# One more level of static start-up: every preparation part as a table step, first key stacks from GpSimd, chunk 0's gate later

## The reference

```
x += (softmax((LN(x) Wq + bq)(ctx Wk + bk)^T / sqrt(32)) (ctx Wv + bv)) Wo + bo      # 16 heads of 32
chosen = argmax(LN(x) gate_w^T)                                                     # 8 experts
x += LN(x) expert_w[chosen]^T
```

## Time and profile before

| | us |
|---|---|
| median of three runs | 1016.04 |
| lowest, highest | 1012.83, 1017.89 |
| profiled execution | 1020.97 |
| its span, first to last instruction | 1019.2 |

### The profile page before, as it was taken

One profiled execution on the slowest core, in us unless ns is written; L12 is line 12 of the kernel. 1 busy time (PEld: TensorE's weight loads), 2 busy tenths in 40 slices (PEclk: granted clock), 3 DMA queues, 4 the chain that ended last, 5 costly groups with the idle time before them and its releaser, 6 DMA issues. The chain is left out here.

```text
span 1019.2 us, 27541 instructions
## 1 busy us (share of the span) xinstructions
PE 922.2 (90%) x8838; PEld 549.9 (54%) x8839; DVE 793.0 (78%) x1828; ACT 558.6 (55%) x928; POOL 540.9 (53%) x553
## 2 busy tenths in 40 slices
PE   5759699999989999989999999999783999999996
PEld 3234555655556555655566555656662555555553
DVE  7746888998979889888899998978876556565663
ACT  4355476776847768658686686774833112121210
POOL 3022445456454654645556555464443577777774
PEclk9877799999989999989999999999886999999998
DMA  9211134244342441533414343224624355555550
GB/s 319 76 41 33 33 95 136 53 135 109 86 135 59 136 136 45 141 82 114 140 43 134 86 119 116 61 75 139 228 108 153 110 166 175 160 169 170 167 179 26
DMA packets 82792, 119.52 MB, mean 117 GB/s; under 512 B 22001, under 2 KB 47141, under 8 KB 82671
## 3 DMA queue, kind: packets, MB, share of 16 engines
q1 hardware_dynamic: 69935, 81.87, 29.9%
q0 software_dynamic: 11664, 36.05, 9.3%
q10 hardware_dynamic: 1072, 0.02, 0.1%
HBM read 55.24 MB, written 38.13 MB: 92 GB/s over the span
## 5 line engine op out<-in xcount | busy, mean ns | idle before, releaser
L527 POOL TENSOR_TENSOR p_lo<-pf,p_hi 77x512 f16<-77x512 f32 x128 | 151.7, 1191 | 222.3 <-ACT p_hi L1085 221.9
L1084 ACT ACTIVATE pf<-scoresT,exp_scale 77x512 f32<-77x512 f32 x256 | 175.2, 684 | 85.6 <-PE scoresT L818 78.3
L1567 PE MATMUL mo<-e_w,x2T_hi 128*128 x576 | 184.4, 382 | 0.7 <-DVE x2T_lo L1604 0.7
L1085 ACT ACTIVATE p_hi<-scoresT,exp_scale 77x512 f16<-77x512 f32 x256 | 175.6, 686 | 0.0
L1587 ACT ACTIVATE x2T_hi<-mt 128x512 f16<-128x512 f32 x72 | 43.1, 598 | 183.5 <-PE mt L1556 183.5
L1614 DVE SCALAR_TENSOR_TENSOR res<-mo,inv,row 128x512 f32<-128x512 f32 x72 | 54.0, 750 | 91.1 <-PE mo L1567 88.9
L527 DVE TENSOR_TENSOR p_lo<-pf,p_hi 77x512 f16<-77x512 f32 x128 | 109.5, 871 | 11.0 <-ACT p_hi L1085 9.5
L1172 DVE TENSOR_REDUCE negmax<-work 128x4 f32<-128x308 f32 x256 | 112.4, 467 | 0.4 <-PE work L870 0.3
L1567 PE MATMUL mo<-e_w,x2T_lo 128*128 x288 | 109.9, 382 | 0.0
L1538 POOL DMA_INDIRECT out<-res,row x72 | 71.5, 994 | 65.0 <-DVE xn L1599 56.8
L790 PE MATMUL work<-xnT_hi,wq_hi 128*128 128x512 f16 x256 | 99.1, 387 | 4.3 <-DVE xnT_lo L1150 2.5
(11 more groups left out here) (256 smaller groups left out, 2205.1 us busy)
## 6 DMA issues: line engine op xcount, KB each, us to landing
row<-rows_by_expert SPq DMA_DIRECT2D x72, 257.5 KB
q_st<-q_hi SPq DMA_DIRECT2D x256, 64.0 KB, 2.0
xt<-in_x SPq DMA_DIRECT2D x15, 1024.0 KB, 8.6
q_st<-q_lo SPq DMA_DIRECT2D x128, 64.0 KB, 2.0
ebuf<-in_L_ffn_expert_w SPq DMA_DIRECT2D x14, 512.0 KB, 7.4
er<-in_L_ffn_expert_w SPq DMA_DIRECT2D x7, 1024.0 KB, 15.1
out<-res,row POOLq DMA_INDIRECT x72, 2.7
xt<-in_x SPq DMA_DIRECT2D x4, 256.0 KB, 6.2
```

Of the source, the lines that this page charges most:

```text
L527: return tt.tensor_tensor(pp[1][0:LK, g % 2, j, :], pf[:, j, :], pp[0][0:LK, g % 2, j, :], ALU.subtract)
L1084: nc.scalar.activation(pf[:, j, :], sbank[n % SB][0:LK, :], ACT.Exp, scale=exp_scale[0:LK, :])
L1085: nc.scalar.activation(pp[0][0:LK, g % 2, j, :], sbank[n % SB][0:LK, :], ACT.Exp, scale=exp_scale[0:LK, :]).then_inc(sem("exp_done"), 1)
L1567: ins = nc.tensor.matmul(obank2[u % 2][:, :], x2T[ia][:, u % 2, k, :], w, start=k == 0 and n == 0, stop=k == KT - 1 and n == 2)
```

## The change

- `prologue()` of TensorE, VectorE and ScalarE is cut into steps (CX, K, CG; Z, VC, KZ, GM, GT, CM, CB, BQ, ST, SA, MQ, MK, MA; PZ, CA, KE, XN) that stand in new tables of iteration -1 among the old ones. GpSimd gets LN, VO, KD in iteration -1 and TR (tables of ranks) in 0.
- The tables of iterations -1 and 0 are new in their order. DV2/DV3, CV move from -1 to 0 (VectorE), BV, WO0, EX0, EX1 from 0 to -1 (ScalarE).
- The gate of chunk 0, before GX in iteration -1, is GY, the first step of iteration 0.
- The stacked keys of batch 0 are issued by GpSimd (KD, behind F), and query pair 1 of chunk 0 by SyncE behind nmT's DMA of iteration 0.
- `ln` makes rstd first and std last, by a multiplication; GX and GY wait for it (`std_ready`).
- e_sum has sixteen columns, EM is gone; one reduction over sixteen columns stands in H of iteration 13.

```diff
-    M12 V00 V01 O2 M13 B2 Q2 R EM0 V10 V11 M20 SL P30 Q3 V20 M21 M22 M23 V21 P31 O3 M30 B3 GX VE V30 M31 M32 M33 V31
+    M12 V00 V01 O2 M13 B2 Q2 R V10 V11 M20 SL P30 Q3 V20 M21 M22 M23 V21 P31 O3 M30 B3 GX VE V30 M31 M32 M33 V31
...
 STEPS_FIRST = order("""
-    T0 T1 AT T2 T3 AB DV1 Q0 DV2 Q1 M00 M01 M02 M03 BT Q2 M10 M11 M12 M13 BB Q3 M20 M21 M22 M23 DV3 GX M30 M31 M32 M33
+    CX0 CX1 K0 K1 K2 K3 T0 AT T1 T2 AB CG DV0 T3 DV1 Q0 BT M00 M01 Q1 M02 DV2 M03 M10 M11 BB Q2 Q3 M12 M13 M20 DV3 M21
+    M22 M23 M30 M31 M32 M33
 VECTOR_FIRST = order("""
-    T0 T1 AR T2 T3 AS WQ0 WQ1 WQ2 WQ3 KL Q0 OM0 OM1 OM2 OM3 BM L0 Q1 M00 M01 M02 M03 BR L1 Q2 M10 M11 M12 M13 BS GS L2 L3
-    Q3 M20 M21 M22 M23 LE GX DV0 M30 M31 M32 M33 DV1 DV2 DV3 CV
+    VC0 Z KZ VC1 CM CB ST0 ST1 GM ST2 ST3 MQ0 BQ SA MQ1 MQ2 MQ3 OM0 MK MA L0 AR OM1 L1 AS T0 T1 L2 GT T2 WQ0 T3 OM2
+    OM3 L3 BM WQ1 Q0 M00 KL BR LE WQ2 M01 Q1 M02 M03 WQ3 BS M10 GS M11 DV0 Q2 DV1 Q3 M12 M13 M20 M21 M22 M23 M30 M31
+    M32 M33
 SCALAR_FIRST = order("""
-    T0 T1 T2 T3 WQ0 KH WQ1 WQ2 WQ3 Q0 Q1 Q2 DV0 Q3 DV1 DV2 DV3 X0 X1 X2 X3
+    PZ0 CA KE0 KE1 KE2 KE3 XN0 XN1 XN2 T0 T1 T2 XN3 WQ0 T3 KH BV WQ1 Q0 WQ2 PZ1 WQ3 Q1 X0 DV0 Q2 DV1 Q3 EX0 X1 DV2 X2
+    EX1 WO0 X3
 GPSIMD_FIRST = order("""
-    KC F
+    LN VO KC F KD
 STEPS_ZERO = order("""
-    NM S00 S01 T0 T1 S02 S03 T2 T3 S10 Q0 S11 M00 S12 M01 DW0 DW1 Q1 PV0 S13 M02 DW2 DW3 M03 M10 S20 S21 M11 M12 DT
-    M13 S22 S23 Q2 DG S30 S31 PV1 M20 Q3 S32 M21 DB S33 M22 PV2 M23 DK M30 GX PV3 M31 M32 M33
+    GY NM DW0 T0 T1 T2 T3 S00 S01 DW1 DW2 S02 DW3 S03 Q0 S10 S11 M00 PV0 M01 S12 M02 Q1 S13 S20 DT M03 S21 M10 PV1 S22
+    M11 M12 S23 Q2 M13 DG S30 S31 Q3 M20 M21 DB S32 M22 S33 M23 PV2 M30 DK M31 GX M32 M33 PV3
 VECTOR_ZERO = order("""
-    NM T0 T1 P00 P01 T2 T3 WO0 Q0 WO1 M00 M01 DW0 DW1 L0 L1 P10 P11 Q1 M02 WO2 DW2 DW3 M03 L2 M10 EM0 M11 L3 M12 LE
-    P20 P21 V00 V01 DT M13 EM1 WO3 Q2 DG V10 V11 M20 P30 Q3 EM2 V20 M21 DB M22 M23 V21 P31 DK GB M30 GX V30 M31 M32 EM3
-    M33 V31
+    GY NM DV2 DW0 DV3 T0 T1 WO0 T2 T3 P00 P01 DW1 DW2 CV L0 DW3 Q0 WO1 M00 P10 L1 V00 M01 M02 Q1 P11 V01 L2 P20 DT M03
+    M10 P21 M11 V10 L3 M12 WO2 LE Q2 M13 DG P30 P31 Q3 M20 M21 V11 WO3 DB M22 M23 V20 M30 DK V21 M31 GX M32 M33 V30
+    V31 GB
 SCALAR_ZERO = order("""
-    S00 S01 T0 T1 S02 S03 T2 T3 WO0 S10 S11 Q0 WO1 S12 S13 Q1 WO2 EX0 S20 S21 WO3 S22 S23 Q2 EX1 DG X0 BV S30 S31 Q3 EX2
-    S32 X1 X2 S33 X3 EX3
+    DV3 WO1 T0 T1 T2 T3 S00 S01 S02 S03 Q0 S10 WO2 S11 S12 Q1 S13 S20 S21 S22 WO3 S23 Q2 S30 DG S31 Q3 EX2 X0 S32 S33
+    X1 X2 EX3 X3
 GPSIMD_ZERO = order("""
-    P02 P03 P12 P13 F P22 P23 P32 P33 A0 A1 A2 A3
+    P02 P03 P12 P13 P22 F P23 P32 P33 TR A0 A1 A2 A3
...
-    e_sum = sb("e_sum", [P, 2])
+    e_sum = sb("e_sum", [P, 2 * E])
...
-    def load_keys(sp, b, dst, name):
-
-        for part, half in ((0, 0), (1, 0), (2, 1)):
+    def load_keys(eng, b, dst, name, parts=range(3)):
+
+        for part in parts:
+            half = part // 2
             for j in range(HG):
                 src = k_nat[half][j * DK:(j + 1) * DK, :, bass.ds(b, 1), :].rearrange("p g a s -> p (g a) s")
-                sp.dma_start(dst[part * DK:(part + 1) * DK, j:H:HG, :], src).then_inc(sem(name), 16)
+                eng.dma_start(dst[part * DK:(part + 1) * DK, j:H:HG, :], src).then_inc(sem(name), 16)
...
+            def stack_queries(i, g):
+
+                if i.is_(-1) and g >= 2:
+                    return
+                if g % 2 and not i.is_(-1):
+                    wait_alone(sp, "scores_ready", H * i.n + (g + 1) * HG)
+                if g % 2 or i.static:
+                    sp.wait_ge(sem("work_used"), use(i, "Q", g) + 1)
+                if g % 2:
+                    stack_pair(g // 2)
+
+            def stack_pair(pair):
+                for part, half in ((0, 0), (1, 1), (2, 0)):
+                    for j in range(HG):
+                        sp.dma_start(
+                            q_st[part * DK:(part + 1) * DK, 2 * pair * HG + j:2 * (pair + 1) * HG:HG, :],
+                            q[half][j * DK:(j + 1) * DK, 2 * pair:2 * pair + 2, :])\
+                            .then_inc(sem(f"q_stacked{pair}"), 16)
 
...
+                if i.is_(0):
+                    sp.wait_ge(sem("work_used"), use(i.plus(-1), "Q", KT - 1) + 1)
+                    stack_pair(1)
...
-                nc.gpsimd.tensor_tensor(std[:, n.slot % 2, :], ve[:], pows[:, 1, :], ALU.pow)
                 do(nc.gpsimd.tensor_tensor(rstd[:], ve[:], pows[:, 0, :], ALU.pow))
                 do(nc.gpsimd.tensor_tensor(nmr[:], mv[:, :, 0], rstd[:], ALU.mult))
                 nc.gpsimd.tensor_scalar(nmr[:], nmr[:], -1.0, None, ALU.mult).then_inc(sem("factors_ready"), 1)
+                nc.gpsimd.tensor_tensor(std[:, n.slot % 2, :], ve[:], rstd[:], ALU.mult).then_inc(sem("std_ready"), 1)
...
+            def value_ones():
+                pool.wait_ge(sem("v_zero"), 2)
                 nc.gpsimd.memset(v_all[0][:, :, :, DK], 1.0).then_inc(sem("v_clear"), 1)
...
+            def rank_tables():
+                pool.wait_ge(sem("k_built"), 1)
+                do = steps(pool, "pool_tables")
...
+            def first_stacks():
+                pool.wait_ge(sem("k_now_clear"), 1)
+                load_keys(nc.gpsimd, 0, k_now, "keys_first", range(2))
+                pool.wait_ge(sem("k_lo"), 1)
+                load_keys(nc.gpsimd, 0, k_now, "keys_first", range(2, 3))
...
+                    n = i.slot if kind == "GY" else i.plus(1).slot
+                    dve.wait_ge(sem("std_ready"), 1 if kind == "GY" else i.n + 2)
...
+                if i.is_(NCHUNK - 3):
+
+                    dve.wait_ge(sem("e_summed"), 2 * E)
+                    nc.vector.tensor_reduce(mx_e[:], e_sum[:], X, ALU.max).then_inc(sem("e_maxed"), 1)
...
-                if not i.is_(0) or k >= 2:
-                    act.wait_ge(sem("e_maxed"), sum_number(i, k) - 1)
-                nc.scalar.activation(ebuf[par][:], src, ACT.Abs, accum_out=e_sum[:, par:par + 1])\
+                if not i.before_loop or k >= 2:
+                    act.wait_ge(sem("e_summed"), sum_number(i, k) - 1)
+                nc.scalar.activation(ebuf[par][:], src, ACT.Abs, accum_out=e_sum[:, bass.ds(sum_number(i, k), 1)])\
...
-            def piece_max(i, k):
-                par = sum_par(i, k)
-                dve.wait_ge(sem("e_summed"), sum_number(i, k) + 1)
-                nc.vector.tensor_tensor(mx_e[:], mx_e[:], e_sum[:, par:par + 1], ALU.max).then_inc(sem("e_maxed"), 1)
-
...
```

More of the change, by code:

```diff
@@ L199, in is_, with before_loop @@
         return self.static and self.n == k
+    @property
+    def before_loop(self):
+        return self.static and self.n <= 0
     def steps(self, table=STEPS):
@@ L583, in iteration @@
                     if kind == "Q":
-                        g, = at
-                        if g % 2 and not i.is_(-1):
-                            wait_alone(sp, "scores_ready", H * i.n + (g + 1) * HG)
-                        if g % 2 or i.static:
-                            sp.wait_ge(sem("work_used"), use(i, "Q", g) + 1)
-                        for part, half in ((0, 0), (1, 1), (2, 0)) if g % 2 else ():
-                            for j in range(HG):
-                                sp.dma_start(
-                                    q_st[part * DK:(part + 1) * DK, (g - 1) * HG + j:(g + 1) * HG:HG, :],
-                                    q[half][j * DK:(j + 1) * DK, g - 1:g + 1, :])\
-                                    .then_inc(sem(f"q_stacked{g // 2}"), 16)
+                        stack_queries(i, *at)
                 if i.is_(NCHUNK - 1):
@@ L678, in iteration @@
                         pool.wait_ge(sem("k_hi"), 1)
+                        pool.wait_ge(sem("std_ready"), 1)
+                        pool.wait_ge(sem("v_clear"), 1)
                         build_k(nc.gpsimd, 0)
+                    elif kind == "LN":
+                        ln(Chunk(0, 0))
+                    elif kind == "VO":
+                        value_ones()
+                    elif kind == "TR":
+                        rank_tables()
+                    elif kind == "KD":
+                        first_stacks()
                     elif kind == "F":
@@ L785, in scale_step @@
                         .then_inc(sem("b_spread"), 1)
+            first = {"CX": context, "CG": gate, "K": keys, "DV": value_heads}
             def product(dst, a, bm, first=True, final=True):
@@ L1026, in sum_piece @@
                 src = ebuf[par][:]
-                if i.is_(0) and k >= 2:
+                if i.before_loop and k >= 2:
                     act.wait_ge(sem(f"e_in{E - 1}"), 16)
@@ L1030, in sum_piece @@
                 else:
-                    loads = 1 if i.is_(0) else i.b * (CPB // 2) + (i.c + 1) // 2 + 1
+                    loads = 1 if i.before_loop else i.b * (CPB // 2) + (i.c + 1) // 2 + 1
                     act.wait_ge(sem(f"e_pre{par}"), 16 * loads)
-                if not i.is_(0) or k >= 2:
```

(15 more changed lines are left out.)

151 lines of the change are left out of this document (75 added, 76 removed).

## The result

The changed kernel takes **976.52 us** (median of 4 runs, 974.32 to 977.27) against 1016.96 us for the kernel before (4 runs, 1012.83 to 1019.33): ratio 0.9614, 95% interval 0.9586 to 0.9642.

The account below looks back on a forecast made before the run. TensorE was taken to bound the loop, VectorE just behind, with start-up losses in iterations -1 and 0. Terms -9.1 - 0.4 - 13.2 - 0.5 - 2.5 = -25.7 us, carried to the 1016.04 us median, gave 990 us, range 979 to 1004.

Parts of the forecast that it names:

- from P33 to the mark: Last GpSimd p_lo of iteration 0 to iteration 1's mark: 14.5 to 14.0 us, hold by seven additions staying.
- the scores' stage: First scores to the end of P33 in iteration 0: from 49.9 to 36.7 us, minus 13.2.
- the loop: Loop iterations without EM and with cheaper GpSimd factors: minus 2.5 us, within 0 to 9.6.
- The mark of iteration 0: Start to VectorE's scaling of the maxima (nmT) in iteration 0: at 48.9 us instead of 58.03, minus 9.1.
- The walk: Steps of the new tables of iterations -1 and 0 timed with trace durations; 31.8 us for the scores' stage.
- rival C: First scores wait for GpSimd's twelve key loads; 5 us slower, 1021 us, if a load costs 3.6 us; chance 0.04.
- Rival A: Iteration 0 keeps its pace, engines waiting in turn, clock at 0.81: 1003.5 us; chance 0.15.
- Rival B: No long hold of GX's and GB's scalar_tensor_tensor beside the additions: 8 us more gain, 982 us; chance 0.12.
- the cover is TensorE: In the loop TensorE waited for VectorE's reductions only some 0.4 us in a plain turn; 0.2 gain taken each.

Follow-up runs that it names:

- run 10: Changed kernel with the first key stacks issued by SyncE behind its loads again, in place of GpSimd's KD: 976.43 us, ratio 0.9616.
- run 7: Changed kernel with the first eight steps of iteration 0 in the old order, scores S00 to S03 between transposes T0 to T3: 983.59 us, ratio 0.9687.
- run 8: Kernel before with only transposes T0 to T3 put ahead of scores S00 to S03 in iteration 0: 1011.55 us, ratio 0.9967.
- run 16: Kernel before with expert columns, new factor order, transposes ahead of the scores and P31 ahead of DB, without the new prologue: 1004.49 us, ratio 0.9895.
- run 4: Kernel before with VectorE's P31 of iteration 0 moved from behind V21 to ahead of DB: 1014.46 us, ratio 0.9986.
- run 14: Changed kernel with GpSimd's rank tables TR ahead of P33, so the seven additions follow P33 directly: 984.43 us, ratio 0.9703.
- run 15: Kernel before with a waited-for one-element memset on GpSimd between P33 of iteration 0 and the seven additions: 1011.02 us, ratio 0.9956.
- run 12: Hold-only measuring kernel: fine arrival moments, a 16-bit subtraction directly ahead of seven GpSimd additions, or ScalarE copying; only the 32 subtraction trials were held, 8.3 to 9.0 us.
- run 13: Hold-only measuring kernel varying the operation ahead of seven GpSimd additions, 90 trials: only the 16-bit subtraction on 77 partitions locked, 6.6 or 4.8 us.
- run 1: Kernel before with only the expert sums changed: sixteen columns, no EM, one reduction in iteration 13: 1010.01 us, ratio 0.9937.
- run 2: Kernel before with only GpSimd's LayerNorm factor order changed, rstd first and std last by a multiplication: 1010.39 us, ratio 0.9943.
- run 3: Kernel before with both the expert columns and the new factor order: 1011.03 us, ratio 0.9948.
- run 17: Changed kernel with std taken first again by a power in GpSimd's factor operations, std_ready kept: 975.54 us, ratio 0.9603.
- run 11: Changed kernel with GpSimd's addition A2 put between P02 and P03 in the 15 iterations of the general table: 976.21 us, ratio 0.9624.
- run 6: Changed kernel with VectorE's P31 moved from ahead of the seven GpSimd additions to behind GX, where they run: 979.87 us, ratio 0.9645.

## Why the prediction was right or wrong

By size, the errors are 7.6 us from P33 to the mark, 4.8 in the scores' stage, about 3 in the loop and 1.6 in iteration -1, all to the same side. Each has its own cause.

**The mark of iteration 0 (predicted 48.9, was 47.35): right within 1.5 us.** The walk held step by step (Q0 at 26.5 us, predicted 27.0; Q2 at 35.9, predicted 37.2): the key products start 0.7 us earlier, the ten reductions end at 46.6 (predicted 48.0), with nothing but GY behind them. Scores at 50.5, predicted 51.7. The keys' twelve transfers took GpSimd 0.55 us each, where 0.69 was assumed (6.62 us in all), and were issued by 43.1 us, long ahead of the scores: rival C had no ground, and run 10 shows that who issues them matters by 0.9 us.

**The scores' stage (predicted 36.7): the mechanism right, the size off.** The walk through the tables gave 31.8 us, measured were 31.9, and that is no luck of the sum: counted from the first score, Q1, Q3, the products of DB and the last exponential each stand within 0.4 us of the walk. What failed is the term put on top of it, 3.4 us for slow stretches of the clock and 1.5 for hand-offs. No run shows these 4.9 us: TensorE waited 1.3 us from the first scores on, and its clock was 0.99 (0.81 before). With the transposes ahead of the scores it has work while the first exponentials run, and the clock stayed at its upper level up to 81.8 us. The lack of waits alone did not keep it there: from 81.8 to 88.6 us the clock was at the lower level, though the trace has TensorE busy without a break from 60 us on, last with the value products and the small ones of the gate. Rival A's premise, a fall after each gap, does not hold either: before, the last fall (111.4 us) came ahead of its gap (112.8 to 120.3), and the gap from 6.0 to 9.1 us was followed by none. Runs 7 and 8 take the order of the steps apart from the rest. The order of eight steps is worth 9.5 us of the stage in the changed kernel and 6.7 in the old one; the rest, 12 us by run 16, is put down by elimination to what else the new tables move (folds, value heads, pair 1 of the queries). How it divides among single steps was not tried. Rival A's outcome is refuted.

**From P33 to the mark (predicted 14.0, was 6.3): wrong, and with it the largest error.** The failed step: "that such an operation is held is shown for p_lo", so GX and GB would be held through all seven additions. That a gate operation can be held so is true (run 4, 7.69 us). But the long hold was no property of seven back-to-back additions. Here it hangs on what runs directly ahead of them: P33, a 16-bit subtraction on 77 partitions that ends as the first addition starts, at 111.1 us. The change put TR between, and the prediction counted TR only as 1.4 us of delay. Runs 14 and 15 show both directions in the kernels (+7.9 us by the medians, +9.0 by the ratios; -3.8 and -4.5), runs 12 and 13 show it outside them. The mark now stands at 88.7 us, amid the additions, which end at 92.1. Rival B had the right size (-8) for the wrong reason, the operation's form: run 4 held that very form.

The prediction weighed here the Trainium skill (SBUF — State Buffer, two separate sides), an exclusive lock of VectorE and GpSimd held for the whole instruction, and set it aside since the trace disagreed. The changed kernel agrees with it (0.79 and 0.62 us, each to the end of the running addition), and so do the trials without the 77-partition subtraction, but for some arrivals in the last 0.05 us of an addition, which waited for one more. The runs behind P33, with 8.98, 7.69, 7.71 and 8.24 us, do not, and neither do the three additions in each iteration of the loop (last section).

**The loop (predicted -2.5): wrong in size.** The failed step is "the cover is TensorE", taken from negmax's row alone. The row beside it, q_lo 3.4 us in 12 iterations, was not read: in the old loop VectorE was late there in every iteration. Either edit by itself removes it, the second adds nothing (runs 1 to 3, 17). Four profiles without either edit have 493.1 to 497.2 us for iterations 1 to 12, twelve with one or both 487.6 to 490.6: a gain of 5 to 6 us. All of TensorE's waits there sum to 16.0 to 19.1 us in the four and 12.0 to 15.2 in the twelve. The 9.5 of the first comparison are partly the scatter of the old kernel's profile. That the two edits' waits would be met and the new reduction cost nothing was right.

## What to carry to other kernels

A hand walk through written orders with durations from the trace was right to 0.4 us in the stage where TensorE was busy nearly throughout, and to 1.5 us in iteration -1; a flat allowance on top of it should be given only where the walk itself shows a gap. A hold that is seen once is to be explained by everything that stands directly around it, the foregoing operation on the other engine included, before it is carried to a changed order; a tiny operation waited for on GpSimd ahead of a burst took under 0.3 us here and made the stage 6.8 us shorter, of which 4 reached the time (run 15). Such holds also stand unseen where another engine covers them (run 11). And when an engine is called covered, sum all its waits in the bound engine's list, not the largest.

## What the runs showed of the hardware that was not expected

- In the trials, a VectorE operation with two SBUF inputs waited for the end of GpSimd's running tensor_tensor and then got in (over 200 trials), but waited for all that followed back to back (up to 8 operations, 9.17 us) if one of them, at its arrival or before, was the 16-bit subtraction on 77 partitions (47 of 47). The 16-bit subtraction on 128 partitions and a 32-bit addition on 77 don't do it. Why is open.
- That subtraction is not the only way to a long hold. In the loop the additions A0, A1 and A2 run back to back behind the indirect DMAs of D. VectorE's p_lo that arrived in A1 never got in at its end: 9 of 9 in the changed kernel (1.79 to 2.53 us) were held to the end of A2, and 129 of 129 in the fifteen profiles with this order of GpSimd's table, that of the kernel before among them (4 of 4). Those that arrived in A2 waited for its end alone. No run tried what does it. GpSimd in the changed kernel, where VectorE's p_lo of run 11 arrived at 135.03 us, 0.75 us ahead of A1's end:

```profile
132.29 0.96 POOL L362 DMA_INDIRECT rows_by_expert<-pay,slot  x1 [0.30 <-issue]
133.28 3.73 POOL L660 TENSOR_TENSOR xt<-xt,bo_rep 128x512 f32<-128x512 f32 x3
```

- GpSimd's own subtractions P02 and P03 let VectorE's p_lo in between them (1.68 us, at 66.67 us of the kernel before). That isn't explained. They may have had a break too short to see, since each waits for its own exponential.
- At an interruption GpSimd's additions lengthen by no more than VectorE's own work: seven took 8.64 us with two 32-element operations let in, 9.10 with one of them and the 77x512 P31 (run 6), against 8.58 with none.
